# The last tile's down products of a gated MLP reordered around their transposes, and split by halves of the output

## The reference

```python
def lora_add(base, inp, A, B):
    Ab = A[layer_idx][lora_indices]
    Bb = B[layer_idx][lora_indices]
    t = jnp.einsum('bri,bni->bnr', Ab, inp)
    return base + jnp.einsum('bor,bnr->bno', Bb, t) * SCALE
gate = lora_add(jnp.einsum('bnh,fh->bnf', x, W_gate), x, A_gate, B_gate)
up = lora_add(jnp.einsum('bnh,fh->bnf', x, W_up), x, A_up, B_up)
act = jax.nn.silu(gate) * up
down = lora_add(jnp.einsum('bnf,hf->bnh', act, W_down), act, A_down, B_down)
...
x = x + _L3_cond_ref(...)
```

## Time and profile before

| what | value |
|---|---|
| median of 3 runs | 1090.57 us |
| lowest, highest run | 1088.47, 1092.51 us |
| the profiled execution: its time | 1087.75 us |
| the profiled execution: its span, first to last instruction | 1085.9 us |
| PE busy | 1054.2 us, 97% of the span |
| the chain of work that ended last | PE 93%, DMA 3%, DVE 2% |
| granted clock of TensorE, mean | 0.998 |

### The profile page before, as it was taken

One profiled execution on the slowest core, in us unless ns is written; L12 is line 12 of the kernel. 1 busy time (PEld: TensorE's weight loads), 2 busy tenths in 40 slices (PEclk: granted clock), 3 DMA queues, 4 the chain that ended last, 5 costly groups with the idle time before them and its releaser, 6 DMA issues.

```text
span 1085.9 us, 18858 instructions
## 1 busy us (share of the span) xinstructions
PE 1054.2 (97%) x6136; PEld 928.8 (86%) x6136; DVE 264.7 (24%) x519; ACT 405.1 (37%) x627; POOL 484.9 (45%) x301
## 2 busy tenths in 40 slices
PE   3999899999999999999999999999999999999997
PEld 3656699988888989999889899899988888998996
DVE  8333112222222222222222122222222221222122
ACT  7002333443443344334434433433343443334331
POOL 0605344545454444455454445444544544454441
PEclk9999999999999999999999999999999999999999
DMA  9798343424243333434242433334241423333320
GB/s 343 253 409 314 105 122 98 121 79 134 73 133 94 103 105 95 127 91 126 71 136 78 120 105 99 111 92 129 88 131 57 144 85 114 105 99 113 107 63 19
DMA packets 100980, 135.49 MB, mean 125 GB/s; under 512 B 26396, under 2 KB 59421, under 8 KB 100957
## 3 DMA queue, kind: packets, MB, share of 16 engines
q1 hardware_dynamic: 100380, 135.12, 39.4%
q10 hardware_dynamic: 576, 0.08, 0.1%
HBM read 118.11 MB, written 16.99 MB: 124 GB/s over the span
## 4 chain that ended last, share of the span: by engine, by line
PE 93%; DMA 3%; DVE 2%; SPq 1%; issue 1%; ACT 0%; DVEq 0%
PE ps L954 45%; PE ps L996 26%; PE ps L964 7%; PE ps L926 5%; PE ps L985 4%; DMA x1p<-yo 2%; PE ps L944 1%; PE ps L1009 1%; PE ps L1008 1%; PE ps L936 1%; PE ps L937 1%; PE ps L939 1%; PE ps L972 1%; SPq L208 0%; DMA tr<-kpad 0%
## 5 line engine op out<-in xcount | busy, mean ns | idle before, releaser
L954 PE MATMUL ps<-wg_hi,x_hi 128*128 128x512 f32 (+2 forms) x768 | 296.6, 386 | 0.4 <-DVE x_lo L795 0.4
L954 PE MATMUL ps<-wg_lo,x_hi 128*128 128x512 f32 (+2 forms) x768 | 291.1, 379 | 0.0
L954 PE MATMUL ps<-wg_hi,x_lo 128*128 128x512 f32 (+2 forms) x768 | 291.0, 379 | 0.0
L464 POOL TENSOR_TENSOR bst<-braw,bst 128x1024 fp32r<-128x1024 f32 (+1 forms) x96 | 213.0, 2219 | 115.7 <-ACT bst L563 115.7
L579 ACT ACTIVATE at_hi<-ps 128x512 fp32r<-128x512 f32 (+1 forms) x96 | 54.0, 562 | 303.3 <-PE ps L985 301.8
L954 PEld LDWEIGHTS ps<-wg_hi,x_lo 128*128 128x128 f32 x768 | 144.7, 188 | 25.5
L954 PEld LDWEIGHTS ps<-wg_hi,x_hi 128*128 128x128 f32 x768 | 144.8, 189 | 22.4 <-issue 0.6
L954 PEld LDWEIGHTS ps<-wg_lo,x_hi 128*128 128x128 f32 x768 | 144.9, 189 | 21.6
L996 PE MATMUL ps<-wd_hi,at_hi 128*128 128x288 f32 (+1 forms) x704 | 155.3, 302 | 1.4 <-DVE at_lo L818 1.4
L996 PE MATMUL ps<-wd_hi,at_lo 128*128 128x288 f32 (+1 forms) x704 | 150.9, 296 | 0.0
L996 PE MATMUL ps<-wd_lo,at_hi 128*128 128x288 f32 (+1 forms) x704 | 150.4, 295 | 0.0
(11 more groups left out here) (142 smaller groups left out, 1090.5 us busy)
## 6 DMA issues: line engine op xcount, KB each, us to landing
braw<-in_tb SPq DMA_DIRECT2D x256, 128.0 KB, 2.7
braw<-in_tb SPq DMA_DIRECT2D x128, 96.0 KB, 2.4
adraw<-in_tad SPq DMA_DIRECT2D x128, 88.0 KB, 1.9
tr<-kpad SPq DMA_DIRECT2D x16, 512.0 KB, 6.8
x1p<-yo SPq DMA_DIRECT2D x16, 512.0 KB, 5.3
xb<-in_x SPq DMA_DIRECT2D x32, 256.0 KB, 2.8
agraw<-in_ta SPq DMA_DIRECT2D x128, 64.0 KB, 1.9
bdraw<-in_tbd SPq DMA_DIRECT2D x128, 64.0 KB, 2.2
```

The source lines that it names most:

```text
L464: sub(v, b_from(p, q), v.bitcast(F32), ALU.subtract).then_inc(s["blo"], 1)
L954: last = mm(bank[:, 0:n], x3s[a][:, k, :], wgs[b][:, k, o:o + n], start=(k == 0 and a + b == 0), stop=False, skip_group_check=True)
```

## The change

It touches only what stands behind the last tile, and the last tile's own `down(t, p, 1)`, which moves there. On PE the four transposes of group 2 now stand after the first two of group 1's four blocks. Their high and low parts go to `x3_hi` and `x3_lo`, the operands of the tile's gate and up products, the last of which were issued before (`at_end`); `ats` can thus still be read by the other two blocks of group 1. Group 2's down products are no longer issued with the two halves in turn: first all four blocks of half 1, then two blocks of half 0, the adapter's transpose, and the last two blocks of half 0 (`down_half`).

```diff
+        def at_end(n):
+
+            return x3s[n][:].rearrange("p k n -> p (k n)")
...
-            def a_high(t, q):
+            def a_high(t, q, to=None):
                 n = PAIRS[q][1] - PAIRS[q][0]
                 act.wait_ge(s["att"], t * 3 + q + 1)
-                copy(ats[0][:, 0:n * P], atp[:, 0:n * P], ACT.Copy).then_inc(s["ahi"], 1)
+                copy((ats[0] if to is None else to)[:, 0:n * P], atp[:, 0:n * P], ACT.Copy).then_inc(s["ahi"], 1)
...
-            a_high(NT - 1, 2)
+            a_high(NT - 1, 2, at_end(0))
...
-            a_low(NT - 1, 2)
+            a_low(NT - 1, 2, (at_end(0), at_end(1)))
...
+            def down_half(h, blocks):
+
+                j0 = PAIRS[2][0]
+                o = NAD + h * DH
+                for j in blocks:
+                    for a, b in PASSES:
+                        last = mm(acc[h], at_end(a)[:, (j - j0) * P:(j - j0 + 1) * P], wds[b][:, j, o:o + DH],
+                                  start=False, stop=False, skip_group_check=True)
+                return last
...
                 if not last:
                     x3_turn(t + 1, 1 - p)
-                down(t, p, 1)
+                    down(t, p, 1)
...
             tile_pe(NT - 1, 1, last=True)
+            j0, j1 = PAIRS[1]
+            down(NT - 1, 1, 1, range(j0, j0 + 2))
             a_turn(NT - 1, 2)
-            down(NT - 1, 1, 2)
+            down(NT - 1, 1, 1, range(j0 + 2, j1))
+            pe.wait_ge(s["alo"], NT * 3)
+            j0, j1 = PAIRS[2]
+            down_half(1, range(j0, j1)).then_inc(s["td"], 1)
+            down_half(0, range(j0, j0 + 2))
             td_turn(NT - 1)
+            down_half(0, range(j0 + 2, j1))
             lora_b_down(NT - 1, 1)
```

More of the change, by code:

```diff
@@ L813, in act_mul, with a_low @@
                 tt(act_t[:, 0:w], act_t[:, 0:w], gub[2 * ((p + q) % 2) + 1][:, 0:w], ALU.mult).then_inc(s["mul"], 1)
-            def a_low(t, q):
+            def a_low(t, q, to=None):
                 n = PAIRS[q][1] - PAIRS[q][0]
+                hi, lo = to or ats
                 dve.wait_ge(s["ahi"], t * 3 + q + 1)
-                tt(ats[1][:, 0:n * P], atp[:, 0:n * P], ats[0][:, 0:n * P].bitcast(F32), ALU.subtract
+                tt(lo[:, 0:n * P], atp[:, 0:n * P], hi[:, 0:n * P].bitcast(F32), ALU.subtract
                    ).then_inc(s["alo"], 1)
@@ L986, in a_turn, with down @@
                 last.then_inc(s["att"], 1)
-            def down(t, p, q):
+            def down(t, p, q, blocks=None):
                 pe.wait_ge(s["alo"], t * 3 + q + 1)
                 j0, j1 = PAIRS[q]
-                for j in range(j0, j1):
+                for j in range(j0, j1) if blocks is None else blocks:
                     m = P if j < FT - 1 else FTAIL
```

## The result

| what | before | changed |
|---|---|---|
| median of 7 runs each | 1090.72 us | 1085.85 us |
| lowest, highest | 1087.93, 1092.51 us | 1083.39, 1087.87 us |
| ratio, 95% interval | | 0.9966, [0.9951, 0.9981] |
| profiled execution: time, span | 1087.75, 1085.9 us | 1087.87, 1086.1 us |

A forecast was written before the change was run, and what follows sets the result against it. PE, busy 97% of the span, bounds the kernel. At most 3.2 us could be gained; three holds take 0.31, leaving 2.90, so the median of 1090.57 becomes 1087.7 us, range 1084.8 to 1091.1.

The forecast's parts named there:

- The holes: Two places near the end where PE waits for ACT and DVE, 1.39 and 1.40 us, which the change fills.
- The hold on the transposes: Last group's transposes, moved forward: their load waits for DVE's product into `act_t`, 0.09 us, between 0 and 0.18.
- The parts: High and low parts of group 2's transposes: the first product using them starts 2.12 us after the transposes start.
- The mask and the spare: DVE's mask after half 1's products ends before the adapter's transpose loads: no wait, 0.14 us to spare.
- The last hold: Low-rank addition's load waits for the adapter's low part until 0.96 us after its transpose's start, held by 0.19 us.
- part 1: Last group's transposes moved between group 1's down products, so group 2's products start earlier: a gain of 1.40 us.
- part 2: Group 2's down products by halves around the adapter's transpose, filling PE's wait before the low-rank addition: gain 1.50 us.
- The bound of 0.7: Rival, chance 0.07: the 24 products by halves pay for 12 new loads, 0.7 us; gain 2.2, time 1088.4.
- the estimate of 1.3 us from the Trainium skill: In group 2's products by halves, 12 more loads on the path take back 1.3 us, leaving a gain of 1.6.
- the rival of one bank: Chance 0.02: group 2's 12 products in a row into one bank await each other; 3.8 us lost, time 1091.5.
- the last sign: Prediction is wrong if the stretches ahead of group 1's first down product, at 1071.89, move by more than the gain.
- a lower level: Rival, chance 0.10: whole runs sit at the profiled execution's level, 2.8 us below the earlier median; median 1084.85.

The follow-up runs named there:

- `turn_only`: Changed kernel with group 2's down products in pairs of halves again, only the transposes moved; ratio to before 0.9988, group 1's first down product to `outb` 9.29 us.
- `halves_only`: Changed kernel with the transposes back behind all of group 1's products, only the order by halves kept; ratio to before 0.999, group 1's first down product to `outb` 9.43 us.
- `same_buffers`: Changed kernel with the last group's parts written into `at_hi` and `at_lo` again, ACT waiting for group 1's products; group 1's first down product to `outb` 9.47 us.
- `after_again`: Changed kernel run once more, unedited; ratio to before 0.9972, group 1's first down product to `outb` 7.89 us.

## Why the prediction was right

- **The holes.** Both were where the chain showed them and both closed; `turn_only` and `halves_only` closed one each, for 1.56 and 1.42 us. The forecast had 1.40 and 1.50.
- **The hold on the transposes.** Forecast at 0.09 with the load's lead kept, so a start at 1.69 after the first down product. They started at 1.59: load and matmul went off 0.02 apart (1076.54, 1076.56), the load held for 0.11. The lead of 0.13 was not paid again after this hold.
- **The parts.** From the transposes' first start to the first product that needs them it took 2.06 (1076.56 to 1078.62), forecast 2.12 with a lower bound of 2.00.
- **The mask and the spare.** Mask 5.54 after the first down product, forecast 5.60; the adapter's transpose at 6.14, forecast 6.21, with no wait.
- **The last hold.** td_lo's end came 0.91 after that transpose's start, and the low-rank addition started 0.96 after it. The forecast had 0.96.
- **The sum.** 2.95 us of stretch against a forecast of 2.90. That it is so close is partly luck, since small errors cancelled: part 1 brought 0.16 more than forecast, as the load's lead was not paid again after a hold, and part 2 some 0.1 less, as the first matmul behind a hold took 0.39 instead of 0.29.
- **The weights by halves.** Products by halves start 0.13 apart, those that load the same part again (1079.11, 1079.25) and those that load another (1078.85, 1078.98), as in pairs, and 18 of them take 2.49 us in either order. The working miscounted the new loads. Of the three passes two share the high part as their stationary operand, so in pairs 8 of the 24 products load weights other than those of the product before, and by halves 16: the change adds 8 such loads and not 12. The row of 352 columns has 8 in its 12 products, not 12. The bound of 0.7 would be 0.5, and the estimate of 1.3 us from the Trainium skill would be 0.9. `halves_only`, with 1.42 of a forecast 1.50, and the equal 2.49 refute both, and the rival of one bank with them. That rival rested on one sentence of the page "TensorE: Matmul & The Clock Gate", in its part on packing small matmuls; the Trainium skill says on the same page, in "Step-by-step: what each phase is for", that the next tile's weights load while this tile's matmul runs, and with that the trace agrees.
- **The signs.** The stretch shortened by 2.95, between 2.4 and 3.3, and PE's holds stayed under 0.2. But the last sign, that the stretches ahead of 1071.89 must not move by more than the gain, came out against the prediction: the changed kernel's profile reaches that place at 1074.97, 3.08 us later. The sign was badly chosen. The same untouched instructions reached it between 1070.32 (`same_buffers`) and 1074.97 in the profiles of the kernels whose start is unedited, at 1072.77 in `after_again`, which is the changed kernel itself. What lies ahead moves with the start of the program, and one profile of each kernel could not test it.
- **The median.** Forecast 1087.7, measured 1085.85. The term that was off is the level of the runs, for which I had only the spread of three: the ratio's 3.7 us hold 2.95 of the change, and the rest lies within its interval. The forecast gave a lower level a chance of 0.10 and did not name its cause; with the executions sorted by mean clock it is plain that most of the spread goes with the clock. That the change itself does nothing to the clock is argued, not shown: the stretches of the start are the same instructions, and in `after_again` the two kernels are 1.5 to 2.9 us apart at equal clock.

## What to carry to other kernels

At the end of a program, where nothing is left to hide a handover behind, split the last block of independent products and put the dependent step's trigger in the middle; count products against the handover's length (here 12 products of 0.133 us for a step of 2.0 less its own 0.36), since one block more or less on either side cost 0.7 to 0.8 us. An early trigger is worth nothing while its result has to wait for a buffer: look for memory that has just become free. To measure such a change, read the stretch between two fixed instructions in the trace; it was 7.89 or 7.90 us in all four profiles with the same end, while the whole executions of these kernels varied by 3.7 to 7.2.

## What the runs showed of the hardware

- An execution's time went with its mean granted clock: 1086.1 us at 1.000 (five executions) and 1091.7 at 0.995 (one), for the same program on the same chip. The falls to 1.2 GHz that the 14 profiles show from 20 us on last a few microseconds and sit in three places near the start, each behind a wait of PE: ahead of the convolution (36 to 44 us, in 3 profiles), in the convolution (80 to 92 us, in 4) and in the first tile (128 to 136 us, in 8). In `turn_only` and `same_buffers` there is none, though PE waited as long in the first tile, 2.3 and 2.5 us. Waits between 2.1 and 2.8 us stand ahead of a fall in some profiles and not in others; what decides it these runs do not show.
- After a hold, a load and its matmul start together (0.00 to 0.02 apart, against a lead of 0.13 in a stream), and the first product of 288 columns takes 0.39 to 0.40 instead of 0.29. The first one behind a transpose does nearly the same without a wait: in the changed kernel the load goes at 1081.11, the product at 1081.13, and it takes 0.38.
- A first silu costs ACT a table load of 1.28 us. With this load done beside other work, and the silu ahead of a copy of 1.15 us, PE's wait of 2.3 us for ACT and DVE went; the two edits were not run apart.
